# Which of two queues issues the second weights and three of the first eight loads, in a conditioned residual kernel

## What is computed

```python
# x: (128, 128, 2048) float32; one index in 0..15 and one in 0..31 per sample
x = x + einsum('bct,bcd->bdt', x, L0_cond_weights[itok_B_0_15])
x = x + einsum('bct,bcd->bdt', x, L1_cond_weights[itok_B_0_31]) \
      + transpose(L1_cond_biases[itok_B_0_31], (0, 2, 1))
return x
```

## Time and profile before

| | |
|---|---|
| median of 3 runs | 639.38 us (639.04 to 639.48) |
| the profiled execution | 638.89 us |
| span in that execution, first to last instruction | 637.1 us |
| granted TensorE clock, mean of the span | 0.994 of full speed |
| PE / DVE / ACT / POOL busy | 86% / 52% / 51% / 20% |
| DMA moved in the span | 271.73 MB, mean 427 GB/s |
| loads of a pair, issue to landing (median) | 24.5 us |
| stores of a pair, issue to landing (median) | 42.9 us |

### The profile page before, as it was taken

One profiled execution on the slowest core, in us unless ns is written; L12 is line 12 of the kernel. 1 busy time (PEld: TensorE's weight loads), 2 busy tenths in 40 slices (PEclk: granted clock), 3 DMA queues, 4 the chain that ended last, 5 costly groups with the idle time before them and its releaser, 6 DMA issues.

```text
span 637.1 us, 6039 instructions
## 1 busy us (share of the span) xinstructions
PE 546.6 (86%) x2334; PEld 237.4 (37%) x2334; DVE 331.6 (52%) x270; ACT 324.5 (51%) x326; POOL 128.2 (20%) x274
## 2 busy tenths in 40 slices
PE   1899999999989888898898988988889889888894
PEld 1344444444334333343343333433433333333331
DVE  1266666666555455544554455445554555455542
ACT  0366666666455455544554455445554455455542
POOL 2322222222122121221211212212112122121101
PEclk9999999999999999999999999999999999999997
DMA  8999999999999999999999999999999999999998
GB/s 358 434 408 433 428 428 431 433 432 428 431 432 432 432 428 432 430 433 431 428 433 433 430 431 427 433 433 431 430 428 434 432 431 429 428 434 433 430 430 350
DMA packets 19297, 271.73 MB, mean 427 GB/s; under 512 B 2565, under 2 KB 2598, under 8 KB 2662
## 3 DMA queue, kind: packets, MB, share of 16 engines
q1 hardware_dynamic: 9504, 137.37, 50.6%
q10 hardware_dynamic: 9398, 132.81, 48.7%
q0 software_dynamic: 384, 1.44, 0.6%
HBM read 137.40 MB, written 134.22 MB: 426 GB/s over the span
## 4 chain that ended last, share of the span: by engine, by line
DMA 65%; PE 30%; DVE 3%; ACT 0%; issue 0%; ACTq 0%; DVEq 0%
DMA out_dram<-xt 40%; PE acc L229 25%; DMA xt<-in_x_dram 23%; PE acc L224 4%; DMA cond_rep<-in_conds_dram 2%; DVE xt L308 1%; DVE xt L307 1%; PE acc L278 1%; ACT L343 0%; ACT spare L372 0%; PE acc L216 0%; ACT both L343 0%; ACTq L325 0%; DVE biasT_even L293 0%; PE acc L218 0%
## 5 line engine op out<-in xcount | busy, mean ns | idle before, releaser
L229 PE MATMUL acc<-xt,both 64*128 64x512 f32 x2048 | 471.9, 603 | 67.7 <-DMA xt<-in_x_dram 65.5
L346 ACT ACTIVATE xt<-acc,bias_of 64x1024 f32<-64x1024 f32 x252 | 279.2, 1108 | 275.8 <-PE acc L229 273.4
L229 PEld LDWEIGHTS acc<-xt,both 64*128 64x128 f32 x2048 | 189.5, 187 | 318.3 <-issue 213.9
L307 DVE TENSOR_SCALAR xt<-acc,bias_of 64x1024 f32<-64x1024 f32 x126 | 160.8, 1276 | 273.0 <-PE acc L229 273.0
L308 DVE TENSOR_SCALAR xt<-acc,bias_of 64x1024 f32<-64x1024 f32 x126 | 162.5, 1290 | 1.8
L179 POOL TENSOR_TENSOR map0T<-w0T_sb,ident 128x128 f32<-128x128 f32 x128 | 65.6, 512 | 466.1 <-PE acc L224 454.2
L224 PE MATMUL acc<-map,map0T 128*128 128x256 f32 x260 | 74.4, 409 | 0.4 <-DVE bias_away L302 0.4
L193 POOL TENSOR_TENSOR map<-w_sb,ident 128x128 f32<-128x128 f32 x126 | 64.5, 512 | 0.0
L224 PEld LDWEIGHTS acc<-map,map0T 128*128 128x128 f32 x260 | 44.5, 191 | 52.5 <-issue 36.9
L343 ACT ACTIVATE both<-acc 128x512 f32<-128x512 f32 x64 | 38.2, 597 | 0.7
L343 ACT ACT_TABLE_LOAD x1 | 1.3, 1283 | 18.7 <-PE acc L224 18.7
(11 more groups left out here) (28 smaller groups left out, 12.2 us busy)
## 6 DMA issues: line engine op xcount, KB each, us to landing
xt<-in_x_dram SPq DMA_DIRECT2D x64, 2048.0 KB, 24.5
out_dram<-xt ACTq DMA_DIRECT2D x63, 2048.0 KB, 42.9
w_sb<-in_w_dram SPq DMA_DIRECT2D x1, 2048.0 KB, 9.5
w0T_sb<-in_w0T_dram SPq DMA_DIRECT2D x1, 1024.0 KB, 5.0
out_dram<-last POOLq DMA_DIRECT2D x2, 512.0 KB, 8.2
out_dram<-last POOLq DMA_DIRECT2D x2, 192.0 KB, 7.6
out_dram<-last ACTq DMA_DIRECT2D x1, 256.0 KB
out_dram<-spare ACTq DMA_DIRECT2D x2, 128.0 KB
```

Of the source, the lines that this page charges most:

```text
L229: return nc.tensor.matmul(acc[:, j * CHUNK:(j + 1) * CHUNK], both[k * HC:(k + 1) * HC, buf, u, k, :], xt[k * HC:(k + 1) * HC, slot, u * T ...
L307: nc.vector.tensor_scalar(to[0:HC, a:a + HALF], acc0[0:HC, a:a + HALF], bias[0:HC, :], None, ALU.add)
L346: return nc.scalar.activation(to[HC:C, v * T + a:v * T + a + HALF], acc1[v * HC:(v + 1) * HC, a:a + HALF], ACT.Identity, bias=bias[v * HC: ...
```

## The change

The second weights and the loads of pairs 1, 3 and 5 are issued by ScalarE, behind its three small loads and ahead of its first wait. SyncE issues the first weights and the other 61 loads. No byte is added or left out, and no wait is added or left out.

```diff
+    ACT_LOADS = (1, 3, 5)
...
         @block.sync
         def _(sp):
             sp.dma_start(w0T_sb[:, :, :], w0T).then_inc(w0_loaded, LOAD)
-            sp.dma_start(w1_sb[:, :, :], w1).then_inc(w1_loaded, LOAD)
             for q in range(PAIRS):
+                if q in ACT_LOADS:
+                    continue
                 slot = q % SLOTS
                 if q >= SLOTS:
                     sp.wait_ge(stored[slot], LOAD * (q // SLOTS))
...
             act.dma_start(cond_rep[:, :], conds[0:1, 1, :].to_broadcast([S1, B])).then_inc(rep_loaded, LOAD)
+            act.dma_start(w1_sb[:, :, :], w1).then_inc(w1_loaded, LOAD)
+            for q in ACT_LOADS:
+                act.dma_start(xt[:, q, :], x_pairs[q, :, :]).then_inc(x_loaded[q], LOAD)
             act.wait_ge(bias_ready, 1)
```

## The result

| | before | changed |
|---|---|---|
| median of 22 runs each | 639.06 us (638.36 to 639.62) | 640.98 us (638.99 to 642.56) |
| the profiled execution | 638.89 us, span 637.1 | 641.74 us, span 639.9 |
| ratio | | 1.0029 (95% interval 1.0023 to 1.0035) |

The change makes the kernel about 1.9 us slower. The forecast was 639.1 and no measurable change; the measured median lies in the stated range but beyond the bound of 0.2% that the forecast set for "the same", on the slower side. The changed kernel also scatters more than before.

A forecast was written before the change was run, and what follows sets the result against it. DMA bounds the kernel at about 431 GB/s. Span 637.1 + 0.5 (late first stores) - 0.7 (end) = 636.9, with 1.8 around it 638.7; runs' median 0.5 higher, 639.2, stated as 639.1 us; range 637.5 to 642.5.

The forecast's parts named there:

- steps 1 to 3, first half: Start: second weights land at 22.6 us, first matmul at 31.5 (10.7 late), first store issued at 44.8.
- step 3, second half: First stores, about 49 to 59 us: hole of 0.1 us plus slow start, +0.5 us taken, bounds 0 and +5.3.
- a rival that needed the weights to land after 22.5 us: At 49 to 59 us: late weights let engines run dry; 643.9 us at the bound, 641.5 at half; chance 0.20.
- step 5: First meeting of store and load, 36 to 38 us: costs 0.5 us before; 0 taken, -0.5 as bound.
- step 4: Long mixed stretch: slots split otherwise, loads about 12.5 us to landing, stores 55, rate unchanged: 0.
- step 6: End: last pair done some 10 us earlier against the end of the data; half of the 1.5 us loss goes, -0.7.
- the second rival: The end closes up: the whole 1.5 us there and 0.5 at the first store-load meeting go, no hole: 637.4; chance 0.15.
- The rule that issuing from several engines saves issuing time only: Whole kernel: transfers from different engines share the same 16 DMA engines; by it alone span 637.1, no change.

The follow-up runs named there:

- the one that waits for pair 2: Kernel before, with GpSimd also waiting for the load of pair 2 before it reads the conditions; no DMA changes queue: 1.0061, 643.22 us.
- the late kernels: Kernels with a delayed first store, such as the kernel before with GpSimd also waiting for the load of pair 1 (1.0013) or pair 2 (1.0061).

## Why the prediction was wrong

1. **The weights, the first matmul, the first store** (steps 1 to 3, first half): right, within 0.5 us each.
2. **The price of the late stores** (step 3, second half): this is the term that failed. It was put at +0.5 us, with +5.3 as bound (its two holes add up to 5.2); measured it is 1.0 MB in 58 to 68 us, 2.3 us, of which 0.5 had been gained before 58, so 1.9 net with rounding. The mechanism was named (the engines run dry because stores enter too late), and it was given to a rival that needed the weights to land after 22.5 us; they landed at 22.3. The working was right up to about 56 us: store 0 alone ran at 422 GB/s in 50 to 54, and load 8 was issued at 56.4, where "about 56" was forecast. What failed is that the time behind it was put at nothing. I looked for the moment at which both queues are empty and took an issued transfer to run at full rate. Load 8 moved 0.03 MB until 60, while 58 to 60, the end of store 1, ran at 246 GB/s; then load 8 ran alone at 348 GB/s until 64; and store 2, issued at 61.5, moved 0.03 MB until 66. So the loss is spread over 58 to 66 us, with a transfer out all the time.
3. **The meeting of store and load** (step 5): 0 taken, and right within the bound, but it moved rather than stayed. From 34 to 45 us the changed kernel moved 427 GB/s against 402, and from 45 to 58 it moved 411 against 429, which nearly cancel. The 0.5 us by which it leads at 58 come in the main from the first 34 us (401 against 397 GB/s).
4. **The long mixed stretch** (step 4): right in what it costs, 431 GB/s and nothing. The split was right only at first: load 8 took 12.6 us to land, but the median of SyncE's loads is 17.2, and that of the stores 50.3, not 55.
5. **The end** (step 6): wrong in sign, -0.7 forecast, +0.7 read in one execution. The away stores are issued at 627.3, 12.6 us before the end of the span in place of 8.4, and the rate still falls off over the last microseconds. So a late issue is not what thins out the end; that part of the second rival fell too. What does was not tested, and 0.7 us of one execution is not beyond doubt either: the medians differ by 1.9, which the first 100 us explain by themselves. In the later kernels the end lost more, 1.7 us behind 600 us in the one that waits for pair 2.
6. **The rule that issuing from several engines saves issuing time only** (the Trainium skill, DMA: Bandwidth & Descriptors, Issuing engines are not separate DMA queues): borne out by the kernel in which only the loads of x move (1.0005, with 1 inside its interval). The changed kernel's loss comes from what each queue serves first, and so from when the weights land.

Sum by its own steps: 637.1 + 1.9 + 0.7 = 639.7 for the span, 0.2 short of the 639.9 read, where 636.9 was forecast.

Not settled: why the packets of load 8 are slow when those of store 0, also alone, are not. With the weights alone moved and with five loads on ScalarE's queue they took 0.73 and 0.74 us each in 60 to 64 us, in the changed kernel 0.82; no kernel isolated it. Nor is it shown why the end takes longer in the late kernels. Nor did any version beat the kernel before; moving only the loads of x equals it.

## What to carry to other kernels

In a kernel bound by DMA, the first stores must be in the queue well before the loads that wait for nothing run out: here those ended at about 49 us, a first store at 38 us cost about 0.1%, barely clear of noise (1.0001 to 1.0019), at 43 about 1 us, at 45 to 46 about 2, and from 46.7 on about 4. Before a transfer is moved to another queue, work out when it lands behind what stands there and at half the rate; a small table that all the first results depend on belongs ahead of the bulk in the queue that is served first. A hole is not only the time when nothing is out: sum the bytes of both kernels in equal windows to find it, since the engines' busy share said 0.99 in the changed kernel's hole.

## What the runs showed of the hardware that was not expected

- A transfer issued while another queue's transfer is being served can start late. In the changed kernel load 8 moved 0.03 MB between its issue at 56.4 us and 60 us, and store 2, issued at 61.5, moved 0.03 MB until 66, where the first transfer of the program moved bytes 1 us after its issue.
- One load alone, with nothing queued behind it, ran at 348 GB/s over 4 us with the DMA share above 1, and slower towards its end, while store 0, also alone, ran at 422, and the loads at the start, with others queued behind them, at 432.
- Small loads beside big ones are slow: in the changed kernel the bias rows and the repeated conditions, 16 KB each, took 9.4 and 10.8 us to land in ScalarE's queue beside SyncE's first weights. Put behind the first weights in SyncE's queue, beside a ScalarE queue full of 16 KB rows, they landed 16.8 and 18.3 us after their issue.
